# A second ScalarE pass that puts rows of y into a PSUM bank for VectorE's subtraction, in layer 0 of a three-layer graph convolution

## The reference

```python
def _gcn_conv(x, W, b, src, dst, norm, n_nodes):
    xw = x @ W
    msg = xw[src] * norm[:, None]
    out = segment_sum(msg, dst, num_segments=n_nodes)
    return out + b
# norm = dinv[src] * dinv[dst], dinv = 1 / sqrt(number of edges that end in the node)
h = _gcn_conv(x, W1, b1, ...)
h = _gcn_conv(h, W2, b2, ...)
h = _gcn_conv(h, W3, b3, ...)
x = _layernorm(x + h)
```

## Time and profile before

| | |
|---|---|
| time, median of 3 runs | 2620.52 us (2619.89 to 2631.47) |
| the profiled execution: its own time | 2630.77 us |
| the profiled execution: span | 2629.0 us |
| granted TensorE clock, mean over the span | 0.911 |
| busy share of the span | PE 81%, PE weight loads 45%, DVE 56%, ACT 30%, POOL 61% |
| mean busy share of the 16 DMA engines in 40 slices of the span | 0.5 to 0.8 |

### The profile page before, as it was taken

One profiled execution on the slowest core, in us unless ns is written; L12 is line 12 of the kernel. 1 busy time (PEld: TensorE's weight loads), 2 busy tenths in 40 slices (PEclk: granted clock), 3 DMA queues, 4 the chain that ended last, 5 costly groups with the idle time before them and its releaser, 6 DMA issues. The chain is left out here.

```text
span 2629.0 us, 32953 instructions
## 1 busy us (share of the span) xinstructions
PE 2116.6 (81%) x10212; PEld 1183.8 (45%) x10212; DVE 1468.8 (56%) x3674; ACT 793.1 (30%) x1502; POOL 1600.1 (61%) x1680
## 2 busy tenths in 40 slices
PE   6734767888888877778898989898778999999985
PEld 6311223444444432234555655555445655555542
DVE  8425664666666653334444544445646666666666
ACT  0402443333343332222332323233322222222311
POOL 0375655656666666645666666666466666666664
PEclk9857787989999999988999999999889999999987
DMA  7756666767777777656777777777767777888876
GB/s 251 256 166 179 220 217 178 212 203 212 219 231 226 241 213 222 208 167 179 218 214 211 211 228 230 229 245 222 238 202 225 240 236 235 258 260 250 253 241 191
DMA packets 286714, 580.98 MB, mean 221 GB/s; under 512 B 72915, under 2 KB 132240, under 8 KB 286544
## 3 DMA queue, kind: packets, MB, share of 16 engines
q0 software_dynamic: 131344, 429.32, 55.0%
q1 hardware_dynamic: 155200, 149.59, 17.5%
HBM read 511.68 MB, written 67.06 MB: 220 GB/s over the span
## 5 line engine op out<-in xcount | busy, mean ns | idle before, releaser
L1028 POOL DMA_INDIRECT ring<-y_dram,kept x1632 | 1571.1, 963 | 904.3 <-issue 438.6
L2242 DVE SCALAR_TENSOR_TENSOR acc<-ps,acc 128x512 f32<-128x512 f32 x494 | 340.8, 690 | 491.0 <-PE ps L1374 223.5
L1255 PE MATMUL ps<-ring,onehot 128*32 128x512 f32 x3264 | 480.7, 647 | 20.1 <-DMA ring<-y_dram,kept 16.4
L1374 PE MATMUL ps<-dense_first,wide_a 128*128 128x512 f32 x1144 | 333.0, 413 | 63.1 <-DVE acc L2242 33.7
L1374 PEld LDWEIGHTS ps<-dense_first,wide_a 128*128 128x128 f32 x1144 | 217.7, 196 | 161.8 <-issue 70.4
L1627 ACT CAST wide_a<-onehot 128x512 fp32r<-128x512 uint8 (+1 forms) x297 | 172.4, 592 | 348.4 <-PE ps L1374 148.7
L1995 DVE TENSOR_TENSOR onehot<-ps,kept 128x128 f32<-128x128 f32 x408 | 115.6, 285 | 275.0 <-remote 193.5
L1374 PE MATMUL ps<-dense_next,wide_a 128*128 128x512 f32 x820 | 243.3, 406 | 25.3 <-DVE acc L2242 13.4
L1374 PE MATMUL ps<-dense_first,y_rows 128*128 128x512 f32 x756 | 221.7, 416 | 25.4 <-DVE acc L2242 11.7
L1331 PE MATMUL ps<-ring,onehot 128*128 128x245 bf16 x494 | 101.4, 296 | 143.8 <-issue 84.4
L1297 PE MATMUL ps<-w,w_sb 128*128 128x512 f32 x368 | 190.5, 666 | 22.8 <-issue 22.8
(11 more groups left out here) (294 smaller groups left out, 2452.3 us busy)
## 6 DMA issues: line engine op xcount, KB each, us to landing
onehot<-a_dram SPq DMA_DIRECT2D x456, 64.0 KB
ring<-y_dram,kept POOLq DMA_INDIRECT x1632, 5.4
y_dram<-acc SPq DMA_DIRECT2D x99, 256.0 KB
a_dram<-ring SPq DMA_DIRECT2D x19, 784.0 KB
acc<-in_x_dram SPq DMA_DIRECT2D x1, 12288.0 KB
y_dram<-acc SPq DMA_DIRECT2D x12, 1024.0 KB
out_dram<-acc SPq DMA_DIRECT2D x48, 256.0 KB
w_sb<-in_x_dram SPq DMA_DIRECT2D x24, 256.0 KB
```

Of the source, the lines that this page charges most:

```text
L1028: pool.indirect_dma_start(ring[:, s, :], None, y_dram[layer], bass.IndirectOffsetOnAxis(ap=rows, axis=0)).then_inc(done, 16)
L1255: mm = pe.matmul(ps[at:at + WIDE, g % BANKS, :], wide_hot[:, r, k, :], ring[:, RING_ORDER[r] * CPQ + k, :], start=opens, stop=closes, tile ...
L1374: mm = pe.matmul(ps[:, bank, :], wide_slots[n % WIDE_SLOTS][:, P * k:P * (k + 1)], y_parts[(TILES * (layer - 1) + tile) % YSLOTS][:, part, :],
L2242: dve.scalar_tensor_tensor(out=rows, in0=ps[:, UNIT_BANKS[n % len(UNIT_BANKS)], :], scalar=0.5, in1=rows, op0=ALU.mult, op1=ALU.add).then_ ...
```

## The change

Three parts, all in layer 0. The two splits of a pair no longer share a quad: the odd one comes one quad later (the first two pairs stay together in quad 41). For each of the 45 splits that are alone in their quad (`staged0`), ScalarE copies the same rows a second time, after the cast, in full precision into PSUM bank 5, once it has kept the quad's first window and the subtraction before is done; VectorE's subtraction waits for that copy and reads the bank in place of SBUF. And from window 104 on TensorE's `build_window` waits until the subtractions of the quads before have been made (for a second window of a quad that has units: those of the quad itself as well), as bank 5 is written again.

```diff
-    SPLIT0_QUAD = [UNITS0_FROM - 2 if b < 2 else LOAD0_QUAD[b] + 1 for b in range(PAIRS0)]
+    SPLIT0_QUAD = [UNITS0_FROM - 2 if k < 2 * PAIR else LOAD0_QUAD[k // PAIR] + 1 + k % PAIR for k in range(TILES)]
...
+    def staged0(k):
+        return k >= 2 * PAIR and len(splits0_at(SPLIT0_QUAD[k])) == 1
+
+    def splits0_by(q):
+        return sum(at <= q for at in SPLIT0_QUAD)
...
-            def build_window(w):
+            def build_window(w, splits=0):
                 pe.wait_ge(win_hot, w + 1)
+                if w >= EARLY_WINDOWS and splits > 0:
+                    pe.wait_ge(split0_ready, splits)
...
                     for w in windows[:1]:
-                        build_window(w)
+                        build_window(w, splits0_by(q - 1))
...
                     if not units:
                         for w in windows[1:2]:
-                            build_window(w)
+                            build_window(w, splits0_by(q - 1))
...
                     for w in windows[1 if units else 2:]:
-                        build_window(w)
+                        build_window(w, splits0_by(q))
...
-                act.copy(y0_high[k % Y0_SLOTS], y0_raw[k % Y0_SLOTS] if k in LOADED0 else tile_of(source0(k))).then_inc(high0_ready, 1)
+                rows = y0_raw[k % Y0_SLOTS] if k in LOADED0 else tile_of(source0(k))
+                act.copy(y0_high[k % Y0_SLOTS], rows).then_inc(high0_ready, 1)
+                if staged0(k):
+                    q = SPLIT0_QUAD[k]
+                    act.wait_ge(split0_ready, k)
+                    act.wait_ge(win_kept, sum(window_quad(w) < q for w in range(WINDOWS)) + len(windows_at(q)[:1]))
+                    act.copy(ps[:, BUILD_BANK, :], rows).then_inc(y0_staged, 1)
...
                 dve.wait_ge(high0_ready, k + 1)
-                dve.tensor_tensor(y0_low[k % Y0_SLOTS], y0_raw[k % Y0_SLOTS] if k in LOADED0 else tile_of(source0(k)),
+                rows = y0_raw[k % Y0_SLOTS] if k in LOADED0 else tile_of(source0(k))
+                if staged0(k):
+                    dve.wait_ge(y0_staged, sum(staged0(j) for j in range(k + 1)))
+                    rows = ps[:, BUILD_BANK, :]
+                dve.tensor_tensor(y0_low[k % Y0_SLOTS], rows,
                                   y0_high[k % Y0_SLOTS].bitcast(F32),
                                   ALU.subtract).then_inc(split0_ready, 1)
```

## The result

The changed kernel takes 2645.01 us, the median of 19 runs (2630.86 to 2661.71). The kernel before, 19 times on the same chip, takes 2626.18 (2610.76 to 2632.07). The ratio is 1.0074, with a 95% interval of 1.0059 to 1.0089: slower by 0.0074 x 2626 = 19 us. The forecast was +16 us and 2636 us; the time and the change both lie inside what was given.

A forecast was written before the change was run, and what follows sets the result against it. PE, DVE and ACT, handing work around in a ring, were taken to bound the stretch, GpSimd having reserve. Wait +16, ACT +3, move -3, contention 0 gave +16 us: 2636 us from the 2620.52 median; 8-in-10 range 2614 to 2660.

The forecast's parts named there:

- The operations: Layer 0 splits: subtraction reading PSUM costs zero extra; copy 0.58 us each, 26 us more on ACT, mostly covered.
- for ACT I had +3 us: The 45 added copies cost time only where PE waits for ACT's widening, 10 times; bounds 0 and 6 us.
- for the move I had -3: Putting the odd splits of 22 pairs one quad later nearly cancels; bounds a 13 us gain or loss.
- Contention: Gathers beside the subtraction: relief shortens POOL's busy time by at most 5.3 us, none reaching the end; taken as zero.
- the 22 us between a gather and its use: Quads 48 to 126: rows are gathered some 22 us before their sum, taken as GpSimd's reserve.
- The quad-by-quad table: Subtraction's end against PE's next window at 45 splits: 36 late by 38 us, seven two-window quads holding 15.
- the nominal 38 us: Total lateness of PE's windows behind subtractions; about 21 after PE's lag, of which three quarters, 16 us, kept.
- PE's lag: PE's work runs behind its records, some 2.5 us at one window, so queued work covers part of the wait.
- Absorbed: Rival: waits fall where PE lags its records or DVE is last; +2 to +8 us, 2625; chance 0.28.
- Uncovered: Rival: the engines' loop has no room, all 38 us and ACT's 6 stay; +44, 2664; chance 0.14.
- The other side: Rival: DVE's quad ends are relieved, 13 us, and POOL's 5.3 us come through; -18, 2602; chance 0.13.
- the forecast's own: Main case: whole kernel slower by +5 to +30 us, 2625 to 2650; chance 0.45.

The follow-up runs named there:

- Run 4: Changed kernel without copy or PSUM input: odd splits moved, PE's windows still wait for the subtractions; 2641.16 us, 1.0059 of the kernel before.
- run 1: Changed kernel with only the odd splits moved one quad later; no copy, PSUM input or PE wait; 2627.15 us, 1.0011 of the kernel before.
- run 2: Changed kernel with odd splits moved and an ACT copy into unread SBUF that nobody waits for, no PE wait; 2630.06 us, 1.0009 of the kernel before.
- run 3: Changed kernel with odd splits moved; the subtraction waits for an ACT copy of the rows but reads SBUF, no PE wait; 2627.46 us, 1.0005.
- run 7: Changed kernel with 38 splits staged, in one-window quads only; no second window waits for its own quad's split; 2249.28 us, 0.9977 of the kernel before.
- run 8: Kernel before plus three GpSimd memsets ahead of the gathers of each of 83 quads; 2308.73 us, 1.0243 of the kernel before.
- run 5: Changed kernel without copy or PSUM input, odd splits moved, only each quad's first window waits; 2252.76 us, 0.9990 of the kernel before.
- run 11: Repeat, on another chip, of the kernel with 38 one-window splits staged and no second window waiting for its own quad; 2251.34 us, 0.9984.
- run 6: Changed kernel without copy or PSUM input, odd splits moved, only second windows of quads with units wait; 2260.08 us, 1.0025 of the kernel before.
- run 9: The whole changed kernel as it is, beside a kernel before of 2254.83 us; 2267.27 us, 1.0062.

## Why the prediction was right, and where it was off

**The cause** was named: the wait for bank 5 ahead of PE's windows. Run 4 shows it beside a kernel before of 2626 us, with runs 1 to 3 as its controls. **Sign and size** were right: +16 forecast, +19 measured, the stretch +16.5 by one profile, the layers behind it nearly unchanged.

**The operations** cost nothing, as taken: 598 ns for the copy where 577 was the bound from its twin, 685 for the subtraction. "Nothing" means within some 8 us: for ACT I had +3 us and runs 2 and 3 give 1.0009 and 1.0005 with intervals up to 1.0028; for the move I had -3 and run 1 gives 1.0011 (0.9990 to 1.0032). The runs can tell neither term from zero. They cancel in the sum, so neither helped nor hurt it.

**Contention.** The gathers' mean in the stretch fell from 967 (306.62 / 317) to 948 ns (299.54 / 316), near the 950 that was named, and POOL's busy time by 7.1 us there. The Trainium skill (SBUF — State Buffer, Who interferes with whom) has a GpSimd instruction that reads SBUF contend with a VectorE one that reads two operands from SBUF and, outside VectorE's two-port modes, not with one that reads at most one. The traces agree. In the kernel before, 19 gathers of the stretch begin while a subtraction with two SBUF inputs runs, and they take 1269 ns in the mean; in the changed kernel 28 begin while one with a PSUM input runs, and they take 945. In run 7 the gather at 427.10 shows it, 1.28 us among neighbours of 0.95. "None of it reaches the end" held beside the kernel of 2626 us. It is not a fact of the kernel: it would have been wrong as a ground on the 2255-us chip, where run 8's added load came through. Nor were the 22 us between a gather and its use a reserve: in run 7, where GpSimd hardly waits, the gathers of a quad still end 8 to 20 us before that quad's mark at nine places between the quads 57 and 125. On these chips the relief may be worth something. Runs 7 and 5 differ in the 38 copies and PSUM inputs, and in no wait of weight. Run 5's POOL from 400 to 800 us:

```profile
L1036 POOL DMA_INDIRECT ring<-y_dram,kept x316 | 305.4, 967 | 96.3 <-issue 93.2 <-PE ps L1263 3.0
```

Its gathers take 967 ns where run 7's take 954. Over 319 gathers that is 4.1 us, and the times differ by 2252.76 - 2249.28 = 3.5 us. The traces place it too. The gathers go four to a quad; from the first of quad 53 to the first of quad 132 it is 401.3 us in run 5, 397.7 in run 7 and 396.9 in run 11, and what follows is 140.4 to 140.5 us to quad 160 in all three. So what copies and PSUM inputs gain on this chip is most likely the relief of the gathers. No run took their length alone, and the fifth of a percent by which run 7 beats the kernel before has the 0.10% of run 5 in it, whose source is open.

**The quad-by-quad table.** At quad 84, the one two-window quad that it shows, it is right: 2.2 us worked out, 2.69 - 0.51 = 2.18 measured. Summed over the seven second windows, PE's idle by the records directly before the window is 6.3 us in the kernel before and 20.9 in the changed one, +14.6 against the 15 that the prediction gave to them. One sign was missed: PE's waits before windows, on the subtraction or unnamed, were to rise by 20 to 40 us, and rise from 34.9 to 42.3 + 3.6 = 45.9, by 11 us (single executions scatter: the same rows give 16.6 in run 1).

**The step that was mis-sized is the split of the sum.** I gave 15 of the nominal 38 us to the second windows, let 21 remain after PE's lag, and kept three quarters, so that the first windows would carry part of the +16. Beside the kernel of 2255 us the first windows alone carry nothing (run 5, 0.9990) and the second windows alone 5.6 us (run 6), of 14 for the whole change. And at their place the seven cost more than their idle, not three quarters of it: the seven two-window quads with the quad behind each, summed from the marks, take 91.8 us in run 9 and 73.6 in run 7, 18 us more for 14 us more of idle (17.4 against 3.0). The lower clock follows some of the stops: in run 9 the granted clock over two-window quad and next is 0.90, 0.88, 0.88 and 0.90 at the quads 55, 90, 113 and 119 and 1.00 at the other three, in run 7 it is 1.00 at all seven. The remaining quads then give back 332.0 - 325.1 = 7 us, presumably because the other engines had worked on meanwhile. So on that chip two errors, too much for the first windows and too little for the second, would cancel in the sum. Whether they are why the sum came out near beside a kernel of 2626 us, for which it was made, is open: how the two kinds share the cost there was not run. Its profiles don't decide it. The same 14 quads take 85.0 us before, 83.1, 90.2 and 88.2 in runs 1 to 3, 92.5 with the wait alone and 95.9 with the whole change, so they scatter by 7 us without the wait; and there the idle time before the first windows that follow a split grows as well, from 15.8 us before and 9.1 to 13.5 in runs 1 to 3 to 18.2 in run 4 and 25.8 with the whole change. That the size came out so near (+16 for +19) is therefore in part luck.

**The rivals.** "Absorbed" (+5) falls by the lower end of the interval, 15 us. "Uncovered" (+44) falls too: 23 us is the upper end; the part of it that came true is its remark on the clock. "The other side" falls by run 1, in which DVE's quad ends are relieved and no window waits, and by run 3. Its second half, that the relief of the gathers comes through, is what runs 7 and 11 suggest for the chips of 2255 us.

**Chances.** With 19 us the case was the forecast's own (+5 to +30), and "slower by over 0.5%" had 0.48.

## What to carry to other kernels

Don't price a new wait by how often it is late: beside a kernel before of 2255 us, 38 splits whose subtraction is waited for in the next quad cost nothing, though PE did idle for them; with seven more whose subtraction is waited for in the same quad, where VectorE makes it last, the change costs 14 us. What decided was the lead that PE had in freeing slots of the ring: as long as it lasted, a stop of PE was free. If a bank is to be borrowed, it is borrowed where its owner is not due again in the same step; run 7 does that and is faster than both kernels, by 0.2% beside a kernel before of 2255 us (it was not run beside one of 2626). And a reserve read from waits belongs to the chip on which the trace was taken; a load added to the engine, as in run 8, is the cheap way to see whether it is one.

## What the runs showed of the hardware that was not expected

**The chips differ by 18%.** The kernel before takes 2626 us on the chip of runs 1 to 4, 2255 on three others and 2668 on a fifth. The difference is not the granted clock alone. The stages view from 400 to 800 us, run 1 beside the kernel of 2626:

```profile
400.00:800.00 400.00, 327.21 (x1492) 168.55 (x1491) 250.52 (x656) 150.65 (x320) 251.03 (x261) 0.94 0.72 211
```

Run 5 beside the kernel of 2255:

```profile
400.00:800.00 400.00, 367.69 (x1794) 195.88 (x1794) 297.23 (x785) 182.30 (x382) 304.01 (x316) 0.99 0.85 262
```

In the same 400 us one chip makes 261 gathers and the other 316, 21% more, at a clock 5% higher; all engines are busier. What the traces show beside it is PE's lag. In the kernel before, on the chip of 2626 us, ScalarE stands idle ahead of 41 windows of the stretch, and 17 of these it begins to keep more than 0.5 us after the matmul has ended by the records, eleven of them more than 2.3 us ("remote" stands as releaser of these). In the traces from the chips of 2255 us none of some 50 is late by more than 0.04 us. Whether that lag is work of PE that the records show too early, or the signal, stays open.

**A wait can cost more than itself where it stands.** 2.2 us of added idle on PE made a quad 3.7 us longer, through some 3.3 us at the lower clock level behind it (run 9 against run 7, quad 55). Over the whole stretch part of that came back.

**The share of the loss is the same on unlike chips:** 0.74% (0.59 to 0.89) where GpSimd waits 91 us of 500 for PE, 0.62% (0.48 to 0.76) where GpSimd is last. The expectation of 0.999 to 1.002 for run 9 came from taking "GpSimd is last" to mean that PE's stops are free. They are free only as long as PE's lead lasts, in run 9 up to the gathers of quad 101.

What stays open: how much of the gain of runs 7 and 11 over the kernel before is the move (no run of it fell on a chip of 2255 us) and how much the relief of the gathers; why the chips differ; and how first and second windows share the cost beside a kernel of 2626 us.
